# Experts of a decoder layer: transposes and the down product amid the gate and up product, and scatters that wait for other experts' scatters only

## What is computed

```python
x = x + _L0_attn_ref(_layernorm(x), ...)
x = x + _L0_xattn_ref(_layernorm(x), ctx_2048, ...)
x = x + _L0_ffn_ref(_layernorm(x), L0_ffn_Wg, L0_ffn_W1, L0_ffn_W2, L0_ffn_W3, L0_ffn_bias)

# _L0_ffn_ref, x as [4096, 512], 8 experts, 2 for each token
routing_weights = sigmoid(x @ Wg.T)
_, top_k_index = top_k(routing_weights + bias, 2)
top_k_weights = take_along_axis(routing_weights, top_k_index, axis=1)
top_k_weights = top_k_weights / top_k_weights.sum(axis=-1, keepdims=True)
expert_w = einsum('tk,tke->te', top_k_weights, one_hot(top_k_index))
h1 = einsum('th,efh->tef', x, W1)          # f = 256
h3 = einsum('th,efh->tef', x, W3)
g = silu(h1) * h3 * expert_w[:, :, None]
out = einsum('tef,ehf->th', g, W2)
```

## Time and profile before

| | us |
|---|---|
| median of 3 runs | 3120.33 |
| lowest, highest | 3118.97, 3124.33 |
| the profiled execution, its own time | 3115.19 |
| its span, first to last instruction | 3113.6 |
| TensorE, VectorE, ScalarE, GpSimd busy | 2689.0, 1919.4, 1348.5, 1013.4 |
| tiles of the experts: first row load issued, last scatter issued | 2699.2, 3105.0 |

### The profile page before, as it was taken

How to read it: one execution, slowest core, us unless ns; L and a number is a source line. 1 busy time by engine, 2 the same in 40 slices (tenths; PEclk the granted TensorE clock), 3 DMA queues, 4 the chain that set the end, 5 groups by cost and what they waited for, 6 DMA issues and landing times. The chain is left out here.

```text
span 3113.6 us, 49696 instructions
## 1 busy us (share of the span) xinstructions
PE 2689.0 (86%) x15042; PEld 1824.7 (59%) x15043; DVE 1919.4 (62%) x3963; ACT 1348.5 (43%) x2725; POOL 1013.4 (33%) x1157
## 2 busy tenths in 40 slices
PE   7999999999999999983888888888888434399997
PEld 6888888888888888862333333333333122166664
DVE  6555555666555555545887778787777278344443
ACT  4333334444343333331666766676666322122221
POOL 1111111222111111123344554555454346422222
PEclk9999999999999999995898999999999666699999
DMA  3111001121111110015677777776776254455554
GB/s 109 41 40 40 33 12 36 40 82 68 41 41 40 40 40 32 10 55 94 92 126 130 129 126 122 133 124 123 125 134 103 61 217 153 156 95 95 98 96 76
DMA packets 140431, 265.49 MB, mean 85 GB/s; under 512 B 39104, under 2 KB 42048, under 8 KB 138832
## 3 DMA queue, kind: packets, MB, share of 16 engines
q1 hardware_dynamic: 114016, 201.88, 29.8%
q0 software_dynamic: 22128, 54.43, 9.0%
q10 hardware_dynamic: 4224, 8.39, 0.7%
HBM read 139.43 MB, written 64.90 MB: 66 GB/s over the span
## 5 line engine op out<-in xcount | busy, mean ns | idle before, releaser
L1389 DVE TENSOR_REDUCE b_negmax<-b_ps_s 128x2 f32<-128x1024 f32 x512 | 618.2, 1221 | 175.5 <-PE b_ps_s L1523 170.0
L1264 ACT ACTIVATE b_probs<-b_ps_s 128x1024 f32<-128x1024 f32 x512 | 516.9, 1021 | 251.3 <-PE b_ps_s L1534 249.5
L255 POOL TENSOR_SCALAR probs<-probs,rinv 128x256 f32<-128x256 f32 x256 | 242.1, 946 | 1099.8 <-DVE rinv L407 1099.8
L1523 PE MATMUL b_ps_s<-b_stack 54*128 54x512 f32 x1024 | 235.7, 457 | 106.8 <-DMA b_stack<-b_split 52.6
L289 ACT ACTIVATE probs<-ps_s,negmax 128x128 f32<-128x128 f32 x256 | 94.2, 368 | 478.5 <-DVE negmax L400 478.5
L1545 PE MATMUL b_ps_o<-b_probs,b_v_stack 128*32 128x512 f32 x2048 | 294.6, 649 | 5.2 <-ACT b_probs L1264 5.2
L1534 PEld LDWEIGHTS b_ps_s<-b_stack 56*128 56x128 f32 x1024 | 99.4, 191 | 330.8 <-issue 177.2
L1534 PE MATMUL b_ps_s<-b_stack 56*128 56x512 f32 x1024 | 259.3, 505 | 34.7 <-DVE b_negmax L1389 17.3
L511 PE MATMUL ps_proj<-xT_h,wq_h 128*128 128x512 f32 x512 | 215.8, 422 | 0.0
L2124 POOL DMA_INDIRECT out<-e_y,e_place_int x71 | 110.5, 1556 | 304.1 <-DMA out<-e_y,e_place_int 261.7
L1523 PEld LDWEIGHTS b_ps_s<-b_stack 54*128 54x128 f32 x1024 | 104.9, 201 | 164.5 <-ACT b_probs L1264 78.3
(11 more groups left out here) (269 smaller groups left out, 6786.4 us busy)
## 6 DMA issues: line engine op xcount, KB each, us to landing
b_stack<-b_split SPq DMA_DIRECT2D x288, 128.0 KB
e_row<-rows_by_expert SPq DMA_DIRECT2D x71, 258.0 KB, 2.6
x_in<-in_x SPq DMA_DIRECT2D x16, 1024.0 KB, 7.5
x<-acc SPq DMA_DIRECT2D x16, 1024.0 KB, 5.0
b_out_tiles<-row_sum_inverses SPq DMA_DIRECT2D x64, 256.0 KB
b_stack<-b_late SPq DMA_DIRECT2D x96, 128.0 KB
acc<-in_x SPq DMA_DIRECT2D x8, 1024.0 KB, 5.9
acc<-x SPq DMA_DIRECT2D x8, 1024.0 KB, 5.6
```

The lines of the kernel that those rows point to most:

```text
L255: nc.gpsimd.tensor_scalar(probs[:, s, P:3 * P], probs[:, s, P:3 * P], rinv[:, s, 1:2], None, ALU.mult).then_inc(probs_done, 1)
L1264: nc.scalar.activation(probs[:, k % 2, p, :, :], ps[:], ACT.Exp, scale=0.25).then_inc(e_done, 1)
L1389: nc.vector.tensor_reduce(negmax[:, k, p, :], ps[:], AX.X, ALU.max, negate=True).then_inc(m_reduced, 1)
L1523: ins = nc.tensor.matmul(ps[:, i, :], stack[rows, quad, 0, p, k * P:(k + 1) * P], stack[rows, quad, 1, p, :], start=True, stop=True)
```

## The change

Three things are changed in `run_experts`, and the table for them is made in `route_tokens`.

The order on TensorE. Within the 12 products of tile u, `g_transposes(u - 1)` come ahead of the sixth (`m == 5`), the transposes of x for tile u + 1 ahead of the ninth, and `down(u - 1)` ahead of the twelfth. `xT` gets a second buffer, since `high` of the next tile now writes while products still read. On VectorE `y_copy(u - 1)` moves ahead of `g(u)`.

The expert's number. It is read once for each tile, ahead of the last product of the tile before, into one of two registers that are kept; `expert_of` only copies from them.

The scatters. There are two semaphores now, `y_out[0]` and `y_out[1]`, for even and odd tiles. How far each must have come is read from a new table, `sent_before`: for a tile that opens an expert (or is unused) it counts all scatters before it, for all others it is 16, which two small transfers into `tag` give at the start. `y_copy` waits for the scatter of two tiles before, on its own semaphore.

The diff, without the passing on of `sent_before` as an argument and its allocation (an int32 tile of 128 x 2 x 71):

```diff
@@ -1700,13 +1701,16 @@
         rstd = sb("rstd", [P, TB])
 
         STEPS = T // P
-        NUMS = E + TB + STEPS + TILES
+        HALF_TILES = (TILES + 1) // 2
+        assert TILES == 2 * HALF_TILES - 1
+        NUMS = E + TB + STEPS + TILES + 2 * HALF_TILES
         nums_int = sb("nums_int", [P, NUMS], I32)
         nums = sb("nums", [P, NUMS])
         expert_no = nums[:, 0:E]
         token_in_group = nums[:, E:E + TB]
         times_128 = nums[:, E + TB:E + TB + STEPS]
-        tile_no = nums[:, E + TB + STEPS:]
+        tile_no = nums[:, E + TB + STEPS:E + TB + STEPS + TILES]
+        halves = nums[:, E + TB + STEPS + TILES:]
         region_row = sb("region_row", [P, E])
         next_row = sb("next_row", [P, E])
         token = sb("token", [P, TB])
@@ -1822,6 +1828,8 @@
                     nc.gpsimd.iota(nums_int[:, at:at + count], pattern=[[step, count]], base=0,
                                    channel_multiplier=per_partition).then_inc(numbers, 1)
                     at += count
+                nc.gpsimd.iota(nums_int[:, at:at + 2 * HALF_TILES], pattern=[[16, HALF_TILES], [0, 2]], base=16,
+                               channel_multiplier=0).then_inc(numbers, 1)
 
                 def rstd_of(G):
                     wait_alone(pool, aggr_done, TB * (G + 1), (consts, 11))
@@ -2005,6 +2013,12 @@
                 v.tensor_scalar(tile_used[:], tile_no, first_tile[:, E:E + 1], None, ALU.is_lt)
 
                 then(v.tensor_tensor(tile_first[:], tile_no, tile_first[:], ALU.subtract))
+                then(v.tensor_tensor(tile_opens[:], tile_first[:], tile_used[:], ALU.mult))
+                then(v.tensor_scalar(tile_opens[:], tile_opens[:], 0.0, None, ALU.is_equal))
+                for i in range(2):
+                    then(v.tensor_scalar(sent[:, i, :], halves[:, 1 - i:1 - i + TILES], -16.0, None, ALU.add))
+                    then(v.tensor_tensor(sent[:, i, :], sent[:, i, :], tile_opens[:], ALU.mult))
+                    then(v.tensor_scalar(sent_before[:, i, :], sent[:, i, :], 16.0, None, ALU.add))
                 then(v.tensor_scalar(tile_row[:], tile_expert[:], float(REGION), -float(PAD_ROW), ALU.mult, ALU.add))
                 then(v.scalar_tensor_tensor(tile_row[:], tile_first[:], float(P), tile_row[:], ALU.mult, ALU.add))
                 then(v.tensor_tensor(tile_row[:], tile_row[:], tile_used[:], ALU.mult))
@@ -2053,7 +2067,7 @@
                 in_groups(pe, GROUPS, group)
 
 
-def run_experts(nc, rows, out, w13, w2, ident, tile_expert, tile_expert_int, tile_row_int,
+def run_experts(nc, rows, out, w13, w2, ident, tile_expert, tile_expert_int, tile_row_int, sent_before,
                 KT, FT, FF, H, E, W0, W1, BEST, TOKEN, ROW, TILES, PASSES):
 
 
@@ -2070,11 +2084,12 @@
             return ctx.enter_context(nc.semaphore("e_" + name))
 
         row = [sb(f"row{i}", [P, ROW]) for i in range(2)]
-        xT = [sb(f"xT_{s}", [P, KT, P], F32R) for s in "hl"]
+        xT = [sb(f"xT_{s}", [P, 2, KT, P], F32R) for s in "hl"]
         gate = sb("gate", [P, FF])
         g = sb("g", [P, FF])
         gT = sb("gT", [P, FT, P])
         y = [sb(f"y{i}", [P, H]) for i in range(2)]
+        tag = [sb(f"tag{i}", [P, 1]) for i in range(2)]
         is_best = sb("is_best", [P, 1])
         not_best = sb("not_best", [P, 1])
         best_weight = sb("best_weight", [P, 1])
@@ -2097,7 +2112,7 @@
         gT_done = sem("gT_done")
         y_filled = sem("y_filled")
         y_copied = sem("y_copied")
-        y_out = sem("y_out")
+        y_out = [sem(f"y_out{i}") for i in range(2)]
         which = sem("which")
         meta_done = sem("meta_done")
         place_done = sem("place_done")
@@ -2118,25 +2133,29 @@
             @block.gpsimd
             def _(pool):
                 def add_to_tokens(u, i):
+                    for n in range(2):
+                        at = sent_before[0:1, n, u:u + 1] if isinstance(u, int) else sent_before[0:1, n, bass.ds(u, 1)]
+                        wait_alone(pool, y_out[n], pool.value_load(at, min_val=16, max_val=16 * TILES), (y_copied, 1))
                     wait_alone(pool, y_copied, u + 2, (y_copied, 1))
-                    if not isinstance(u, int) or u:
-                        wait_alone(pool, y_out, 16 * u, (y_copied, 1))
                     nc.gpsimd.indirect_dma_start(out, bass.IndirectOffsetOnAxis(place_int[i][:], 0), y[i][:], None,
-                                                 compute_op=ALU.add).then_inc(y_out, 16)
+                                                 compute_op=ALU.add).then_inc(y_out[i], 16)
 
                 def tile(u, t, i):
                     if not isinstance(u, int) or u:
                         add_to_tokens(u - 1, 1 - i)
 
+                for n in range(2):
+                    nc.gpsimd.dma_start(tag[n][:], ident[:, 0:1]).then_inc(y_out[n], 16)
                 in_steps(pool, TILES, tile, first=4, last=3)
                 add_to_tokens(TILES - 1, (TILES - 1) % 2)
-                pool.wait_ge(y_out, 16 * TILES)
+                for n in range(2):
+                    pool.wait_ge(y_out[n], 16 + 16 * len(range(n, TILES, 2)))
 
             @block.scalar
             def _(act):
                 def high(u, i):
                     act.wait_ge(x_transposed, u + 1)
-                    nc.scalar.activation(xT[0][:], ps_x[i][:], ACT.Copy).then_inc(x_high, 1)
+                    nc.scalar.activation(xT[0][:, i], ps_x[i][:], ACT.Copy).then_inc(x_high, 1)
 
                 def gT_copy(u):
                     act.wait_ge(g_transposed, u + 1)
@@ -2160,7 +2179,7 @@
 
                 def low(u, i):
                     dve.wait_ge(x_high, u + 1)
-                    nc.vector.tensor_tensor(xT[1][:], ps_x[i][:], xT[0][:].bitcast(F32), ALU.subtract).then_inc(x_low, 1)
+                    nc.vector.tensor_tensor(xT[1][:, i], ps_x[i][:], xT[0][:, i].bitcast(F32), ALU.subtract).then_inc(x_low, 1)
 
                 def meta(u, t, i):
 
@@ -2176,9 +2195,9 @@
                     v.scalar_tensor_tensor(weight[i][:], row[i][:, W1:W1 + 1], not_best[:], best_weight[:],
                                            ALU.mult, ALU.add).then_inc(meta_done, 1)
 
-                def y_copy(u, i):
+                def y_copy(u, t, i):
                     if not isinstance(u, int) or u >= 2:
-                        dve.wait_ge(y_out, 16 * (u - 1))
+                        dve.wait_ge(y_out[i], 16 * t + 16)
                     nc.vector.tensor_copy(place_int[i][:], place[i][:]).then_inc(place_done, 1)
                     dve.wait_ge(y_filled, u + 1)
                     nc.vector.tensor_copy(y[i][:], ps_y[i][:]).then_inc(y_copied, 1)
@@ -2186,12 +2205,13 @@
                 def tile(u, t, i):
                     if not isinstance(u, int) or u < TILES - 1:
                         low(u + 1, 1 - i)
+                    if not isinstance(u, int) or u:
+                        y_copy(u - 1, t - 1 + i, 1 - i)
                     dve.wait_ge(gate_done, u + 1)
                     dve.wait_ge(meta_done, u + 1)
                     nc.vector.scalar_tensor_tensor(g[:], ps_h[i][:, FF:], weight[i][:], gate[:], ALU.mult,
                                                    ALU.mult).then_inc(g_done, 1)
                     if not isinstance(u, int) or u:
-                        y_copy(u - 1, 1 - i)
                         dve.wait_ge(place_done, u)
                     if not isinstance(u, int) or u < TILES - 1:
                         meta(u + 1, t + i, 1 - i)
@@ -2200,7 +2220,7 @@
                 low(0, 0)
                 meta(0, 0, 0)
                 in_steps(dve, TILES, tile, first=4, last=3)
-                y_copy(TILES - 1, (TILES - 1) % 2)
+                y_copy(TILES - 1, (TILES - 1) // 2, (TILES - 1) % 2)
 
             @block.tensor
             def _(pe):
@@ -2226,34 +2246,45 @@
                         ins = nc.tensor.matmul(ps_y[i][:], gT[:, f, :], w, start=(f == 0), stop=(f == FT - 1))
                     ins.then_inc(y_filled, 1)
 
-                def expert_of(u):
+                expert = [pe.alloc_register(f"expert{i}") for i in range(2)]
+
+                def load_expert(u, i):
+
                     at = tile_expert_int[0:1, u:u + 1] if isinstance(u, int) else tile_expert_int[0:1, bass.ds(u, 1)]
-                    return pe.value_load(at, min_val=0, max_val=E - 1)
+                    pe.reg_load(expert[i], at)
+
+                def expert_of(i):
+                    return pe.snap(expert[i], min_val=0, max_val=E - 1)
 
                 def tile(u, t, i):
                     first = isinstance(u, int) and u == 0
-                    e = expert_of(u)
-                    e_before = None if first else expert_of(u - 1)
+                    last = isinstance(u, int) and u == TILES - 1
+                    e = expert_of(i)
+                    e_before = None if first else expert_of(1 - i)
                     pe.wait_ge(x_low, u + 1)
                     m = 0
                     for j in range(KT):
```

(20 more changed lines are left out.)

15 lines of the change are left out of this document (9 added, 6 removed).

## The result

| | before | changed |
|---|---|---|
| median of 4 runs on one chip, us | 3120.43 | 3094.99 |
| lowest, highest | 3118.97, 3124.33 | 3092.47, 3099.73 |
| the profiled execution, its own time | 3115.19 | 3092.47 |
| its span | 3113.6 | 3091.0 |

The ratio is 0.9918, with a 95% interval of 0.9903 to 0.9934: 25 us faster. The forecast was 3097.4 with a range of 3089 to 3110; its sum for the profiled execution, 3092.3, meets 3092.47. That agreement is partly luck, and most of what follows is about which parts of it are.

A forecast was written before the change was run, and what follows sets the result against it. Bound: the row of scatters, 5.49 us a tile, with TensorE's 5.17 floor close behind. Loop 14.4, tail 8.0, start 0.6, number row -0.1 sum to 22.9 us: 3092.3 profiled, 3097.4 median; own range 3090 to 3107, widened to 3089 to 3110.

The forecast's parts named there:

- The wait for other experts' scatters: GpSimd's scatters into `out`: the 5.49 us limit goes for 62 tiles; opening tiles' scatters come about 0.3 late, unseen by TensorE.
- The loop: Tiles 2 to 70 on TensorE: 5.24 us a tile in place of 5.452, 14.4 us gained.
- The stall for `g`: TensorE ahead of the transposes of `g`, after five products: waits 0.07 us a tile, 0.24 at the bad end.
- The read beside the burst: TensorE's read of the expert's number: falls 0.9 us after the scatter's start, not 2.0 to 2.9, so fast.
- The tail: From tile 70's first product to the last scatter: 10.2 us in place of 18.2, 8.0 gained.
- the chain ends 2.4 us before TensorE does: Scatters of the five empty tiles, one by one: 5 x 5.49 = 27.5 us from scatter 65, costing nothing.
- a read behind the landing: GpSimd's reads of two counts, some 0.27 to 1.1 us each, run while its queue waits for `y_copied`: cost nothing.
- The start: Tile 0's transposes for tile 1 come four products (0.9 us) earlier; `gate`'s table load gives some back: 0.6 us gained.
- No read collides: Rival: TensorE's read still meets the scatter's burst, 5.45 us a tile, 3111.7 us; chance 0.10.
- no chain is left: Rival: scatters still follow one another at 5.49 us, nothing gained but the start, 3119.7 us; chance 0.07.
- the stall for `g` is 0.05 and not 0.55: Rival: TensorE waits 0.55 us for `g` ahead of its transposes after the fifth product, 3130 us; chance 0.06.
- The transposes amid products: Rival: TensorE's four transposes a tile don't overlap, 0.275 us each, 5.90 a tile, 3142 us; chance 0.02.

The follow-up runs named there:

- the waits alone: The kernel before with only the scatters' waits changed, old order and both reads at the tile's start kept: 3131.97 us, ratio 1.0041 to the kernel before.
- order and one read: The changed kernel, but each scatter waits for the one before on one semaphore, as before the change: 3105.96 us, ratio 0.9967 to the kernel before.
- `g` after six: The changed kernel with the transposes of `g` ahead of the seventh product and not the sixth: 3099.31 us, ratio 0.9921 to the kernel before.

## Why the prediction was right, and where it wasn't

**The wait for other experts' scatters: right.** The limit went, for 62 tiles. The opening tiles' scatters were put 0.3 late; they start 2.0 us behind `y_copy` where the rest start 0.77 behind, so 1.3 late, since the scatter before takes 5.65 us and not the 4.7 that the prediction took over from the trace of before. TensorE didn't see it, as said.

**The loop: right, term by term.** 5.24 predicted, 5.242 measured; 14.4 and 14.3 us. The stall for `g` was put at 0.07 and is 0.05. What made up the difference, late row loads of some 0.03 a tile, stood nowhere in the prediction: it named the two queues that read registers beside the scatter, but not the transfer of the tile that falls into the same burst. SyncE issues it behind `meta`, and `meta` stood right behind `y_copy` and now has `g` between, while its reader comes four products sooner. I had moved the reader and costed only what it feeds. The trace of before had the price: 3.6 to 4.2 us for a row load issued 1.5 us after a scatter.

**The read beside the burst: right,** and the sharpest part. The read now begins 1.2 us after the scatter (1.0 to 1.5 in eight of ten; 0.9 said) and takes 0.30. That the same mechanism would make the waits alone slower than before was found only by leaving the rest out. The prediction had taken the one read and the order together without asking whether either was enough.

**The tail: the step that failed.** Said: last scatter 10.2 us behind tile 70's first product, 8.0 gained. Measured: 3082.57 - 3067.35 = 15.2, 3.0 gained. TensorE's part was right to 0.1 (`y_copy` of tile 70 ends 9.6 behind that product, 9.68 said). The other leg, "the chain ends 2.4 us before TensorE does", failed twice. First by an index: `down(65)` stands ahead of the last product of tile 66, so `y_copy` of tile 65 ends 0.66 us after tile 67's first product, one tile later than reckoned, and scatter 65 starts at T70 - 14.3 and not at T70 - 19.7: 5.4 us. The prediction's own "+1.5" for a scatter's start gives 14.2. Second by the step: five took 29.6 us and not 27.5. From landing to next scatter they took 0.90, 1.47, 0.74, 1.46 and 0.75 us, not 0.77 each, since every second one has a read behind the landing, which the prediction had put at nothing: 1.5 us. The landings make the other 0.6, with 5.68 us for the first of them. The chain of the five empty tiles is what ends last, and by 5 us.

**The start: wrong.** 0.6 said, 0 measured: tile 2 stands 16.98 us behind the first row load (16.96 before). The transposes did come sooner, and order and one read had the 0.6 (16.35). What took it back goes with the granted clock. The windows view (from:to, us, busy us and instructions of PE, PEld, DVE, ACT, POOL, granted clock, DMA share, GB/s), two lines of before, two of the changed kernel, one of order and one read:

```profile
2702.00:2706.00 4.00, 2.49 (x8) 1.80 (x9) 1.24 (x6) 0.60 (x1) 0.00 (x0) 0.50 0.14 49
2706.00:2710.00 4.00, 3.40 (x14) 2.56 (x12) 0.00 (x0) 0.57 (x1) 0.00 (x0) 0.81 0.25 66
2702.00:2706.00 4.00, 4.00 (x13) 2.88 (x12) 0.69 (x1) 1.99 (x3) 0.00 (x0) 0.61 0.13 41
2706.00:2710.00 4.00, 4.00 (x19) 2.74 (x18) 1.79 (x8) 1.26 (x3) 0.00 (x0) 1.00 0.12 31
2702.00:2706.00 4.00, 4.00 (x14) 3.19 (x15) 0.36 (x3) 0.06 (x1) 0.00 (x0) 0.62 0.23 66
```

From the first row load on, the lower level (0.50, which is 1.2 GHz) lasts some 8.4 us before, 8.6 in order and one read, and 11.2 in the changed kernel. The windows whose middle lies 8.8, 7.5 and 10.1 us behind that load have 0.81, 0.62 and 0.61, in the same order. In the other executions of the changed kernel it lasts 11.2 and 11.4, with tile 2 at 16.97 and 16.87; with `g` after six it lasts 10.4, with tile 2 at 16.70. That the clock is the cause is drawn from these, no run isolates it, and why it rises later is open; TensorE had idled for 36 us until the first tile in before, changed, and order and one read alike.

**The sum.** Said 22.9, measured 22.7 between the profiled executions; but 14.3 of the loop, 3.2 of the tail (counted to the span's end) and 5.2 that has nothing to do with the change took the place of 14.4, 8.0 and 0.6. On the stage alone, 22.9 against 17.4, the prediction was 5.5 too high; that the sum met the measurement is luck.

**The rivals.** No read collides, no chain is left, the stall for `g` is 0.05 and not 0.55. The transposes amid products take 0.11: 2860.31 - 2859.41 above. "TensorE: Matmul & The Clock Gate" of the Trainium skill, part 4, measures about 275 ns for one in a kernel's context. The trace doesn't agree with it here as a distance; 0.27 is the length of one record: four, 0.11 apart, take 0.60 us in all.

## What to carry to other kernels

When a wait is taken out of a chain, its transfers lock to a fixed place of the loop, as they did here: look for everything short that reads or loads in the microseconds behind that place, on every queue, because what collided now and then can come to collide nearly each time. Move one such read first; a new order of the whole loop was not needed here, and brought a late row load that the old one did not have. The price of a collision may stand in the trace of before, where it harms nothing yet. Where a serial chain ends a kernel, count it from its first link in the tile where that link really stands.
